# The Newton step of two layer norms: three VectorE operations in place of five, the square and the epsilon on ScalarE

## The reference

```
def _layer_norm(x, w, b, eps=1e-05):
    mu = jnp.mean(x, axis=-1, keepdims=True)
    var = jnp.mean(jnp.square(x - mu), axis=-1, keepdims=True)
    return (x - mu) * jax.lax.rsqrt(var + eps) * w + b

h = _layer_norm(x, ln1_w, ln1_b)
q, k, v = projections of h by Wq, Wk, Wv      # 4 heads of 32
x = x + causal_attention(q, k, v) @ Wo + bo
nx = _layer_norm(x, ln2_w, ln2_b)
noisy = nx @ Wr + br + noise * softplus(nx @ Wn + bn)
router_out = softmax over the two largest of 8
for e in range(8):
    expert_out += router_out[..., e:e+1] * (relu(nx @ W1[e] + b1[e]) @ W2[e] + b2[e])
final = where(sigmoid(nx @ Wsk + bsk) <= 0.5, x + expert_out, x)
```

## Time and profile before

| | |
|---|---|
| three runs | 804.17, 804.82, 807.13 us; median 804.82 |
| the profiled execution, its own time | 797.03 us |
| its span, first to last instruction | 795.3 us |
| busy: PE, DVE, ACT, POOL | 575.5, 576.2, 486.8, 415.8 us |
| mean granted TensorE clock | 0.875 of full speed |

### The profile page before, as it was taken

The page is one execution under the profiler, slowest core; times in us unless marked ns, Lnnn a source line. Parts: engine busy times, 40 slices in busy tenths (PEclk is TensorE's granted clock), DMA queues, the critical chain, the costliest instruction groups (busy, mean ns, idle before and its releaser), DMA issues.

```text
span 795.3 us, 31404 instructions
## 1 busy us (share of the span) xinstructions
PE 575.5 (72%) x11012; PEld 450.8 (57%) x11012; DVE 576.2 (72%) x2270; ACT 486.8 (61%) x979; POOL 415.8 (52%) x478
## 2 busy tenths in 40 slices
PE   0468998999998999998756209999999999720000
PEld 0246776776776776676645107777777777610000
DVE  3357878778788888878665626777777777718997
ACT  2357777677787788777654307888888888700000
POOL 3000767767766777777655740666666666630000
PEclk9978999999999999999986558999999999965555
DMA  9854332232332233235453247677666676319998
GB/s 96 239 161 136 90 102 87 75 100 69 93 97 72 89 100 100 65 101 115 106 161 98 89 169 286 230 232 235 234 233 235 231 236 230 124 35 326 331 334 262
DMA packets 147276, 127.32 MB, mean 160 GB/s; under 512 B 37538, under 2 KB 125699, under 8 KB 147232
## 3 DMA queue, kind: packets, MB, share of 16 engines
q1 hardware_dynamic: 110368, 89.99, 37.7%
q10 hardware_dynamic: 24576, 20.98, 8.6%
q0 software_dynamic: 12288, 15.77, 6.2%
HBM read 73.86 MB, written 62.78 MB: 172 GB/s over the span
## 4 chain that ended last, share of the span: by engine, by line
PE 38%; issue 19%; DVE 17%; POOL 12%; ACT 4%; DVEq 3%; DMA 2%; ACTq 2%; SPq 1%; POOLq 1%
POOL expert_rows L1136 11%; PE ps L505 6%; PE ps L548 4%; PE ps L626 3%; PE ps L627 3%; PE ps L628 3%; PE ps L638 3%; PE ps L639 3%; DVE z L1062 3%; PE ps L640 3%; PE ps L570 3%; DVE stats L831 3%; DVE z L1067 2%; PE ps L586 2%; DVE sc_m L874 1%
## 5 line engine op out<-in xcount | busy, mean ns | idle before, releaser
L1136 POOL DMA_INDIRECT expert_rows<-pay,rows_of x256 | 255.4, 998 | 184.8 <-DVE rows_of L930 101.9
L1148 POOL DMA_INDIRECT expert_results<-z,words x128 | 136.3, 1065 | 106.0 <-DVE z L1029 74.7
L676 ACT ACTIVATE z<-xres,shift,rstd 128x128 f32 (+1 forms) x256 | 105.1, 483 | 34.1 <-DVE shift L865 34.1
L1043 DVE TENSOR_TENSOR hlo<-h,hhi 128x512 fp32r<-128x512 f32 x128 | 89.8, 701 | 46.0 <-ACT hhi L789 44.3
L787 ACT ACTIVATE h<-ps,w1x 128x512 f32<-128x512 f32 x128 | 88.3, 690 | 35.2 <-PE ps L628 31.0
L789 ACT ACTIVATE hhi<-ps,w1x 128x512 fp32r<-128x512 f32 x128 | 87.3, 682 | 0.0
L548 PEld LDWEIGHTS ps<-pT,v_sb 32*32 32x32 f32 x4096 | 48.8, 104 | 62.4 <-issue 60.3
L548 PE MATMUL ps<-pT,v_sb 32*32 32x32 f32 x4096 | 59.2, 202 | 31.5 <-DVE sc_m L874 24.0
L505 PE MATMUL ps<-ident,z 128*128 128x128 f32 x256 | 45.3, 305 | 25.1 <-ACT z L676 19.3
L528 PE MATMUL ps<-kT,qT 32*32 32x32 f32 x4096 | 56.4, 201 | 4.6 <-issue 0.5
L638 PE MATMUL ps<-hhi,w2x 128*128 128x512 f32 x128 | 56.5, 442 | 4.2 <-issue 4.2
(11 more groups left out here) (147 smaller groups left out, 1321.1 us busy)
## 6 DMA issues: line engine op xcount, KB each, us to landing
w1x<-split_weights SPq DMA_DIRECT2D x33, 514.0 KB, 3.8
w2x<-split_weights SPq DMA_DIRECT2D x33, 512.5 KB
expert_results<-zeros SPq DMA_DIRECT2D x32, 512.0 KB
pay<-expert_rows SPq DMA_DIRECT2D x33, 264.0 KB, 3.6
xres<-in_r_x SPq DMA_DIRECT2D x32, 256.0 KB
split_weights<-w2x ACTq DMA_DIRECT2D x16, 512.0 KB
hhi<-expert_results SPq DMA_DIRECT2D x16, 512.0 KB, 5.5
hlo<-expert_results SPq DMA_DIRECT2D x16, 512.0 KB, 5.5
```

What stands on the lines that cost most here:

```text
L676: m = nc.scalar.activation(z[:, j:j + 1], tile(xres, n, j), ACT.Identity, bias=shift[:, which, j:j + 1], scale=rstd[:, which, j:j + 1])
L1043: ev.tensor_tensor(hlo[:, c], h32[:, c % 2], hhi[:, c].bitcast(F32), ALU.subtract).then_inc(s_h_lo, 1)
L1136: g.indirect_dma_start(rows, bass.IndirectOffsetOnAxis(ap=rows_of[:, odd, k * J + j:k * J + j + 1], axis=0), pay[:, odd, k, j, :], None, b ...
L1148: g.indirect_dma_start(results, bass.IndirectOffsetOnAxis(ap=words[:, slot, j:j + 1], axis=0), yrow[slot][:, j, :], None, bounds_check=K * ...
```

## The change

Epsilon is added by ScalarE as the bias of the Ln, from a one-column tile that GpSimd fills at the start. ScalarE also squares the guess, with a scale that makes it half the square. VectorE then has three operations: (variance + eps) times half the square; minus 1.5, times guess, which is minus rstd; and -mean times that. Both norms so come out negated, and the scales ln1_w and ln2_w are negated once at the start by VectorE; ScalarE's first wait is now for these two (and no longer for the constants' transfers). NORM falls from 7 to 5.

```diff
+        eps = sb("eps", [P, 1])
-        NORM = 7
+        NORM = 5
+        SQRT_HALF = 0.5 ** 0.5
...
 ScalarE, step:
-                    act.wait_ge(s_norm, (t + 2) * NORM + 3)
-                    nc.scalar.activation(log_var[:, which], var_eps[:, which], ACT.Ln).then_inc(s_norm_log, 1)
+                    act.wait_ge(s_norm, (t + 2) * NORM + 2)
+                    nc.scalar.activation(log_var[:, which], moments[:, which, :, 1], ACT.Ln,
+                                         bias=eps[:]).then_inc(s_norm_log, 1)
                     act.wait_ge(s_norm_log, t + 3)
                     nc.scalar.activation(rstd0[:, which], log_var[:, which], ACT.Exp, scale=-0.5).then_inc(s_norm_r0, 1)
+                    act.wait_ge(s_norm_r0, t + 3)
+                    nc.scalar.activation(half_sq[:, which], rstd0[:, which], ACT.Square,
+                                         scale=SQRT_HALF).then_inc(s_norm_sq, 1)
 ScalarE, start:
-            act.wait_ge(s_consts_in, CONSTS)
+            act.wait_ge(s_norm_signs, 2)
...
 VectorE, step:
-                if norms:
-                    dve.wait_ge(s_norm, base + 2)
-                    ev.tensor_scalar(var_eps[:, which], moments[:, which, :, 1], EPS, None, ALU.add).then_inc(s_norm, 1)
...
-                    dve.wait_ge(s_norm_r0, t + 3)
-                    ev.tensor_tensor(newt_a[:, which], rstd0[:, which], rstd0[:, which], ALU.mult).then_inc(s_norm, 1)
+                    dve.wait_ge(s_norm_sq, t + 3)
+                    ev.scalar_tensor_tensor(newt_b[:, which], moments[:, which, :, 1], EPS, half_sq[:, which], ALU.add,
+                                            ALU.mult).then_inc(s_norm, 1)
+                    dve.wait_ge(s_norm, base + 3)
+                    ev.scalar_tensor_tensor(rstd[:, which], newt_b[:, which], -1.5, rstd0[:, which], ALU.add,
+                                            ALU.mult).then_inc(s_norm, 1)
                     dve.wait_ge(s_norm, base + 4)
-                    ev.scalar_tensor_tensor(newt_b[:, which], newt_a[:, which], -0.5, var_eps[:, which], ALU.mult,
-                                            ALU.mult).then_inc(s_norm, 1)
-                    dve.wait_ge(s_norm, base + 5)
-                    ev.scalar_tensor_tensor(rstd[:, which], newt_b[:, which], 1.5, rstd0[:, which], ALU.add,
-                                            ALU.mult).then_inc(s_norm, 1)
-                    dve.wait_ge(s_norm, base + 6)
                     ev.scalar_tensor_tensor(shift[:, which], moments[:, which, :, 0], -1.0, rstd[:, which], ALU.mult,
                                             ALU.mult).then_inc(s_norm, 1)
 VectorE, start:
+            dve.wait_ge(s_consts_in, CONSTS)
+            for norm in (norm1, norm2):
+                ev.tensor_scalar(norm[:, 0:1], norm[:, 0:1], -1.0, None, ALU.mult).then_inc(s_norm_signs, 1)
 GpSimd, start:
+            g.memset(eps[:], EPS)
```

More of the change, by code:

```diff
@@ L112, in build @@
         moments = sb("moments", [P, 2, J, 2])
-        var_eps = sb("var_eps", [P, 2, J])
+        eps = sb("eps", [P, 1])
         log_var = sb("log_var", [P, 2, J])
         rstd0 = sb("rstd0", [P, 2, J])
-        newt_a = sb("newt_a", [P, 2, J])
+        half_sq = sb("half_sq", [P, 2, J])
         newt_b = sb("newt_b", [P, 2, J])
@@ L227, in build @@
         s_norm_r0 = sem("norm_r0")
+        s_norm_sq = sem("norm_sq")
+        s_norm_signs = sem("norm_signs")
         s_z1 = sem("z1_made")
```

## The result

| | before | changed |
|---|---|---|
| median of the timed runs | 804.82 us (5 runs, 802.09 to 807.13) | 794.3 us (5 runs, 789.62 to 794.53) |
| ratio, 95% interval | | 0.9874 (0.9838 to 0.9909) |
| the same, in a second job | 803.21 us (17 runs) | 787.79 us (6 runs), 0.981 (0.9759 to 0.9861) |
| the profiled execution, its span | 797.03, 795.3 us | 789.62, 787.5 us |

The change makes the kernel 10.5 us faster, 1.3%, and by the second job up to 15. I had predicted 3.6 us, 801.2 us; the measured 794.3 lies just under the range, which began at 795.0. The ratios are of executions in the fast state, each kernel against the kernel before in the same job (one of the 12 executions of `fill_a_before`, at 2715.95 us, is thereby outside them).

The account below looks back on a forecast made before the run. It took a VectorE and TensorE loop as the bound from 66 to 240 us, GpSimd's sends mostly afterwards. Gains of 3.1 + 0.5 = 3.6 us gave 793.4 profiled; with 7.8 us between profile and runs, 801.2 us, range 795 to 806.5.

Parts of the forecast that it names:

- the first stretch: Stage one, 66 to 240 us: a loop of VectorE and TensorE sets the time; 15 steps gain 0.24 us each.
- The start: Kernel start: two sign operations and one more GpSimd fill fall into VectorE's idle time of 5.69 us; cost zero.
- worries about ScalarE: Rival: ScalarE becomes the bound if L702 ends late and Ln and Square cost 0.32; 7.7 us slower, 812.5 us; chance 0.08.
- table loads: Rival: Square is not in the loaded activation set, so 36 steps load twice, 92 us, 897 us; chance 0.01.
- its 1.07: Start of L859 behind the aggregates, in us, if each ScalarE operation cost about 0.3; nearly nothing would be won.
- the term of the second stretch: Stage one, 240 to 363 us: GpSimd sets the pace at 11.47 us a step, so removing L840 gains nothing.
- My 3.1: Gain in us in 66 to 240 us: 15 x 0.24 = 3.6, less 0.5 of lag.
- 0.5 of lag: GpSimd, falling behind 0.17 us a step, still lags two or three steps when the second stretch begins; 0.5 us lost.
- This second term: Sign against the forecast: a changed number of low-clock stretches, each worth 1.6 us; one or two equal half the sum.
- the 7.8 us: Median of the timed runs above the profiled 797.03 us, unexplained; the same amount was subtracted from the runs' median.
- the rival that the whole stage gains: Rival: cheap Ln and GpSimd slack in all steps; up to 32 steps gain 0.24 to 0.33, 7.7 to 10.6 us; chance 0.32.
- cheap Ln of 0.21: Condition of the whole-stage rival: the Ln with bias tile costs 0.21 us, as the present one, for 0.30 forecast.

Follow-up runs that it names:

- fill_a_before: The kernel before with eight matmuls, whose results are unused, put into TensorE's idle time ahead of L548; ratio 1.0022.
- after_again: The changed kernel, run and profiled again without any edit; 787.79 us, ratio 0.981.
- pool_slower3: The changed kernel with one more GpSimd fill of 128x1152 in each routing step; ratio 0.9982.
- square_only: The changed kernel with epsilon added by VectorE again and the Ln without bias tile, the Square staying on ScalarE; ratio 0.9991.
- eps_only: The changed kernel with half the square made by VectorE again, epsilon staying in the Ln as bias; ratio 0.9894.
- pool_faster: The changed kernel with a table of token numbers in place of GpSimd's token addition in each routing step; ratio 0.9867.

## Why the prediction was wrong

**The direction and the place were right, point by point.** The chain L820, aggregates, Newton step, L874, L548 was the pace of the first stretch; the Ln with a bias tile costs 0.30 us, Square 0.21, and the product starts 0.85 us behind the aggregates for 0.86 forecast. The start costs nothing: the changed kernel's early steps begin within 0.5 us of the old ones. The worries about ScalarE and about table loads did not come true: the one table load is still the only one. The rule of the Trainium skill (ScalarE: Activation LUTs, Rules for kernel authors) gives 0.3 us for an ACTIVATE whose bias comes from a one-column tile. The trace agrees for the Ln, which has such a bias, at 0.30; the Square and the Exp have none and took 0.21. The prediction had left that condition out and put all three at 0.3 (and its 1.07 adds up to 1.04).

**The step that failed is the term of the second stretch, which I set to nothing.** It rests on two readings of one profile: that GpSimd is the pace there, with "eight of its steps take 91.79 us, 11.47 each", and that the Ln no longer waits for L840. Both were features of that execution. In the two repeats GpSimd waited for row numbers 5 times and the Ln for L840 9 and 11 times, so the loop was the pace, as in the first stretch; and the nine steps of the second stretch went from 108.3 us on average to 103.9, where I had nothing.

The 11.47 is also no pace of GpSimd's own, but a mean over two kinds of steps. GpSimd's periods there are 11.27 to 11.34 us, and 11.77 to 11.78 three times. In these three the last send lasts 1.46 to 1.47 us and not 0.97. The timelines of the two engines, kernel before:

```profile
294.04 0.68 DVE L923 TENSOR_TENSOR pn<-probs,prec 128x512 f32<-128x512 f32 x1
```

```profile
294.10 1.47 POOL L1136 DMA_INDIRECT expert_rows<-pay,rows_of  x1 [0.30 <-issue]
295.56 0.22 POOL L1129 CAST pay<-token 128x8 uint32<-128x8 f32 x1
```

All three such sends (294.10, 317.15, 340.20) begin 0.06 to 0.07 us behind the start of L923, which reads two tensors from SBUF, and end about 0.5 us late. The same holds wherever it happens: over the 16 profiles at some 800 us, from 95 to 375 us, the 27 sends that begin 0.03 to 0.54 us behind the start of this operation end 1.52 to 1.54 us behind that start, some 0.85 us behind the operation's end, so that they last up to 1.50 us; those that begin from 0.1 us ahead of it to 0.02 us behind it last 0.97 to 1.03. The Trainium skill (SBUF — State Buffer, Who interferes with whom) says that a VectorE instruction with two SBUF inputs contends with a GpSimd instruction that reads SBUF; the trace agrees for the sends that begin second, with these numbers. The sends of the changed kernel's first profile fell outside the costly part of that range, one of its second profile's fell into it (323.38, 1.46 us), and in the two repeats of the kernel before none did up to 375 us, with steps of 11.53 us all the same. So the collisions hid GpSimd's pace in the first profile; they did not make the steps of the kernel before long.

GpSimd's undisturbed pace is 11.28 us, and the loop, once 0.25 us shorter, has short steps of 11.20 to 11.28. It does not meet a wall 0.07 us below its old 11.54 but one 0.25 us below. The changed kernel has come to that wall: in `after_again` GpSimd's sends are the chain of the second stretch, and seven of its periods there are 11.26 to 11.34 us. No run moves L923 alone; what is said of the collisions is read off the timelines.

**The sum redone.** Over the 24 steps the profiles of the kernel before take 284.4, 291.0 and 288.7 us, mean 288.0; the changed one's 278.5 and 277.4, mean 278.0. Of these 10 us, short steps explain 24 x (11.53 - 11.245) = 6.8 us. My 3.1 stood for 15 of them at 0.24, less 0.5 of lag. The rest, and half a us too much, goes with the long steps: 6.3 on average before, 4 after, 2.3 x 1.6 = 3.7 us. The timed runs bear this out. In the job of `after_again` the mean granted clock was 0.880 over the 6 of the changed kernel and 0.870 over the 17 of the kernel before; as the clock is either 1.00 or 0.50, that is about 188 us at the low clock for 209. Among the 17, each us more at the low clock went with 0.27 us more of time, so the 20 us less are worth some 5.5 of the 15 us of that job, by this estimate, and some 10 are left for the shorter steps. The first job's changed kernel had 0.873 and gained 10.5.

**This second term I had only named as a risk.** I had also read the level of the timed runs too lightly: the first profile had 5 long steps and took 797 us, under all the timed runs beside it (though not under those of other jobs, which began at 796 to 797); the two others had 7 at 799.8 and 801.1 us. So the 7.8 us "for a reason no row shows" is at least in part a matter of long steps, and the timed runs, with more of them (mean clock 0.869 to 0.871 in the other jobs, 0.875 in the profile), leave GpSimd more slack than the profile, as the two repeats do. That speaks for the rival that the whole stage gains, to which I gave 0.32 and 794 to 797 us. Its time and its slack came true, its cheap Ln of 0.21 did not, and the last six steps, to which both gave a gain, show none.

**What stays open.** Kernels with shorter steps mostly had fewer long ones (3 to 5 up to 11.35 us, 5 to 8 from 11.4 on, 11 at 11.69), but `pool_slower3` had 8, each count is from one profile, and `square_only` had shorter steps than the kernel before and no less time. Filling the idle time did not lower the count, though the timed runs had a higher mean clock. Why the clock falls less often in the changed kernel, and whether it always does, is not settled.

**A better version?** None that is as exact. `eps_only`, `pool_faster` and the changed kernel cannot be told apart. Without the Newton step the time is 787 us, at most 1% under the changed kernel, where GpSimd runs at its 11.28 us in most steps and TensorE hardly waits for VectorE any more.

## What to carry to other kernels

Before one profile is made to say which engine sets a stretch's pace, take a second one of the same kernel: here the waits and the chain of one stretch changed from execution to execution. Before a pace is taken as an engine's floor, list its periods one by one: a mean over 11.28 and 11.77 hid that the longer ones were collisions, which come and go with the phase of two engines. In a loop of engines that wait for each other, count the time between two events (aggregates done, product starts) and not the operations removed: leaving out one 0.17 us operation that stood ahead of ScalarE's Ln and of the router's operations brought nearly the whole gain, and moving another brought nothing that could be measured. When the profile is faster than every timed run, find the difference first, since it may decide which engine binds.

## What the runs showed of the hardware that I had not expected

- A scattering send of GpSimd that began 0.03 to 0.54 us behind the start of L923, a VectorE operation with two SBUF inputs, ended 1.52 to 1.54 us behind that start (27 of 27 in 16 profiles), so it took up to 1.50 us for 0.97; one that began 0.00 to 0.02 us behind took 0.97 to 0.98.
- A GpSimd fill of 0.47 us between the token's addition and the first send cost nothing, as the issue gap shrank from 0.66 to 0.16 us.
- An Ln whose bias comes from a tile took 0.30 us, the Ln without one 0.21, both on 128x8 elements.
- On one chip the same program took 1034 us for 803, with holes of 0.4 to 1.4 us between single small matmuls of L528, at both levels of the granted clock.
